# Norm in two halves, turned gate products and a lighter VectorE queue in the prologue of an attention and mixture-of-experts kernel

## The reference

```
xn = layernorm(x)
q, k, v = heads(xn @ W.T)                         # 16 heads of 16
std = softmax(causal(q k' / 4)) v                 # plain attention
gauss = exp(-0.5 |q - pos|^2 / scale^2), dirp = tanh((q - pos) . dirn)   # 8 splats a head, same for k
gsa = softmax(causal(q k'/4 + 0.3 * (amp gauss_q gauss_k' + 0.4 * amp gauss_q dirp_q (gauss_k dirp_k)'))) v
attn = ((1-blend) std + blend gsa) @ Wo.T
logits = xn @ gate_w.T                            # 16 experts, top 2, capacity 128
w = sqrt(softplus(logits)); y = sum_k w_k * W2[e_k] (silu(W1[e_k] xn) * (W3[e_k] xn))
shared = Ws2 (silu(Ws1 xn) * (Ws3 xn))
out = x + attn + y + shared
```

## Time and profile before

| | us |
|---|---|
| median of 3 runs | 358.19 |
| lowest, highest | 356.69, 360.31 |
| the profiled execution, whole | 356.44 |
| its span (first to last instruction) | 354.7 |
| PE, DVE, ACT, POOL busy in it | 316.1, 235.8, 201.4, 39.7 |
| mean granted TensorE clock | 0.981 |

### The profile page before, as it was taken

The page is one execution under the profiler, slowest core; times in us unless marked ns, Lnnn a source line. Parts: engine busy times, 40 slices in busy tenths (PEclk is TensorE's granted clock), DMA queues, the critical chain, the costliest instruction groups (busy, mean ns, idle before and its releaser), DMA issues.

```text
span 354.7 us, 6091 instructions
## 1 busy us (share of the span) xinstructions
PE 316.1 (89%) x2064; PEld 161.2 (45%) x2064; DVE 235.8 (66%) x735; ACT 201.4 (57%) x300; POOL 39.7 (11%) x59
## 2 busy tenths in 40 slices
PE   0899898977779999999999999999999999999984
PEld 0548533223423455444544455445445554445352
DVE  4858776499997568964766567665766568666424
ACT  1696277575645576654565465555555545647730
POOL 7300000000020000111111111102110004444000
PEclk9998998999978999999999999999999999999999
DMA  7424353224146303635455536554554443222011
GB/s 243 132 43 65 57 99 88 55 43 67 30 65 167 73 2 48 137 112 138 112 140 116 161 87 146 129 143 100 128 145 134 102 80 78 59 72 60 7 59 59
DMA packets 25790, 33.54 MB, mean 95 GB/s; under 512 B 4636, under 2 KB 18556, under 8 KB 25756
## 3 DMA queue, kind: packets, MB, share of 16 engines
q1 hardware_dynamic: 24056, 28.85, 35.3%
q0 software_dynamic: 1536, 4.20, 4.3%
q10 hardware_dynamic: 164, 0.07, 0.1%
HBM read 16.15 MB, written 4.26 MB: 58 GB/s over the span
## 4 chain that ended last, share of the span: by engine, by line
PE 44%; DVE 5%; ACT 2%; issue 2%; DMA 1%; SPq 1%; DVEq 0%
PE ps L897 12%; PE ps L813 6%; PE ps L822 5%; PE ps L879 5%; PE ps L867 4%; PE ps L775 4%; PE ps L852 2%; DMA stage<-split 1%; PE ps L817 1%; PE ps L870 1%; ACT arena_p L670 1%; DVE mx L1215 1%; ACT small L682 1%; PE ps L826 1%; PE ps L801 1%
## 5 line engine op out<-in xcount | busy, mean ns | idle before, releaser
L670 ACT ACTIVATE arena_p<-ps 128x1024 f32<-128x1024 f32 (+1 forms) x192 | 148.0, 808 | 49.6 <-PE ps L879 29.2
L897 PE MATMUL ps<-arena_p,v_full 128*32 128x512 f32 (+3 forms) x768 | 72.6, 496 | 0.0
L1183 DVE CUSTOM_DVE_ANT_0 ps<-ps,mask_r 128x128 f32<-128x128 f32 (+3 forms) x128 | 61.7, 501 | 11.6 <-PE ps L775 6.9
L775 PE MATMUL ps<-stage 96*128 96x512 bf16 (+3 forms) x160 | 50.6, 354 | 8.1 <-DVE mx L1215 3.7
L867 PE MATMUL ps<-stage 98*128 98x512 bf16 (+1 forms) x192 | 51.6, 333 | 3.7 <-ACT arena_p L670 3.0
L1215 DVE TENSOR_REDUCE mx<-ps 128x1 f32<-128x512 f32 x64 | 43.9, 686 | 14.5 <-PE ps L775 14.1
L879 PE MATMUL ps<-stage 98*128 98x512 bf16 (+1 forms) x192 | 47.2, 334 | 2.5 <-ACT arena_p L670 2.3
L452 POOL DMA_INDIRECT wt<-xn_scratch,ids_sb x16 | 15.3, 954 | 235.3 <-PE ps L801 107.6
L897 PEld LDWEIGHTS ps<-arena_p,v_full 128*32 128x32 f32 x768 | 20.1, 110 | 34.6 <-issue 30.0
L775 PEld LDWEIGHTS ps<-stage 96*128 96x128 bf16 x160 | 15.6, 99 | 29.6 <-issue 22.2
L675 ACT ACTIVATE small<-ps 128x176 f32<-128x176 f32 x24 | 7.6, 317 | 37.2 <-PE ps L813 37.2
(11 more groups left out here) (199 smaller groups left out, 374.2 us busy)
## 6 DMA issues: line engine op xcount, KB each, us to landing
w_sb<-in_w_dram SPq DMA_DIRECT2D x16, 352.0 KB
stage<-split SPq DMA_DIRECT2D x48, 96.0 KB
stage<-split SPq DMA_DIRECT2D x96, 32.0 KB
stage<-split SPq DMA_DIRECT2D x48, 64.0 KB
arena_o<-in_w_dram SPq DMA_DIRECT2D x16, 176.0 KB
ye_scratch<-wt SPq DMA_DIRECT2D x16, 128.0 KB, 2.6
stage<-split SPq DMA_DIRECT2D x32, 48.0 KB
acc<-in_x_dram SPq DMA_DIRECT2D x2, 512.0 KB, 4.7
```

What stands on the lines that cost most here:

```text
L670: A(to, ps[:, 1 + 2 * s:3 + 2 * s, off:CH], ACT.Exp, scale=SCALE).then_inc(done, 1)
L775: ins = M(b[:, 0:n1 - n0], qs[0:KR, pr, h, it * P:(it + 1) * P], ks[0:KR, pr, h, n0:n1], start=True, stop=True)
L897: ins = M(ps[c:c + 2 * HD, 0, off:CH], v_full[:, jb + s, g * GH + h, :], of, start=jb + s == 0, stop=end or last, skip_group_check=last an ...
L1183: return V.tensor_tensor_reduce(row, row, mask_r[:, CH - row.shape[1]:CH], 1.0, NEG, ALU.add, ALU.max, to)
```

## The change

- x arrives in four DMAs of 256 rows. Mean, variance, root and normalisation are done for rows 0 to 511, then for 512 to 1023. One q projection of the first half is put on PE between the transposes of the halves. Waits on ACT's count now go through `emptied_at`.
- The squares of q and k for heads 0 to 7 move from ACT (read from PSUM) to DVE (`square`, four of 128 x 512, read from SBUF).
- The gate products are turned round: `gateT` uses the gate weights as the stationary side (four matmuls of 16 x 512), DVE copies both 16-row blocks to `pv_sb`, and eight small transposes (`gate`, 0 and 1) bring them back to tokens on partitions.
- The third parts of the features (at = 2, 3) move from DVE to GpSimd.
- On DVE, `gate` now stands before the first maximum, `plus_one` after two tasks of the maxima, and a part of the old `plus_one` (`corrected`) in front of the copy of shift 0.
- For the maxima made in the prologue and in turns 0 and 1 (`g <= EARLY`), PE adds the mask by one more matmul of 128 x 128 (48 in all) and DVE uses the plain maximum.
- PE: the first `proj1` stands in front of shift 0; v tasks 2 and 3 stay between the maxima. ACT: the table changes for Ln, Sqrt and Exp are in other places, all before the last two `proj1` are emptied.

```diff
-        PRO = [("xnT", (k, tq)) for tq in range(NC) for k in range(KD)]
-        PRO += [("proj", (s, tc)) for s in range(2) for tc in range(NC)] + [("par", m) for m in range(2)]
-        PRO += [("feat", (tc, w)) for tc in range(NC) for w in range(2)] + [("gate", 0)] + [("v", n) for n in range(NT // 2)]
+        PRO = [("xnT", (0, 0)), ("xnT", (1, 0)), ("proj", (0, 0)), ("xnT", (0, 1)), ("xnT", (1, 1)),
+               ("proj", (1, 0)), ("proj", (0, 1)), ("proj", (1, 1))]
+        PRO += [("par", m) for m in range(2)]
+        PRO += [("feat", (tc, w)) for tc in range(NC) for w in range(2)] + [("gateT", 0), ("v", 0)] + [("gate", tq) for tq in range(NC)]
+        PRO += [("v", n) for n in range(1, NT // 2)]
...
+        EARLY = 1
...
 # GpSimd, after its constants
+            for at in (2, 3):
+                pool.wait_ge(second_rest, at + 1)
+                pool.wait_ge(second_part, at + 1)
+                nc.gpsimd.tensor_tensor(part_of(at, 2), rest_of_x(at), part_of(at, 1), ALU.subtract).then_inc(part_done[at], 1)
...
 # SyncE
-            for n in range(NC):
-                sp.dma_start(acc[:, n * TC:(n + 1) * TC, :],
+            for n in range(NT // 2):
+                sp.dma_start(acc[:, 2 * n:2 * n + 2, :],
...
 # ScalarE
-                if m == 0:
-                    A(sq[m][:, s, cols], b, ACT.Square).then_inc(squares, 1)
...
+            root_of(0)
+            act.wait_ge(norm_ready, 1)
+            A(NRM, NSQ, ACT.Sqrt).then_inc(norm_root, 1)
+            evacuate(("xnT", (0, 0)))
+            evacuate(("xnT", (1, 0)))
+            root_of(1)
+            exponentials()
             evacuate(("proj", (0, 0)))
...
+            evacuate(("v", 3))
+            evacuate(("proj1", (0, 0)))
+            shift_rows(act, -1, 0, 0)
             evacuate(("proj1", (0, 1)))
...
             A(g_[10][:, :, :], g_[11][:, :, :], ACT.Sqrt).then_inc(gate_act, 1)
+
+            A(PRE_, GG, ACT.Exp)
+            evacuate(("proj1", (1, 0)))
             evacuate(("proj1", (1, 1)))
...
 # TensorE
+                elif kind == "gateT":
+                    for k in range(KD):
+                        for tq in range(NC):
+                            last = M(b[32 * tq:32 * tq + E, :], gw_sb[:, k, :], xnT[:, k, tq * CH:(tq + 1) * CH],
+                                     start=k == 0, stop=k == KD - 1)
...
-                                start=True, stop=True)
+                                start=True, stop=g > EARLY)
+                        if g <= EARLY:
+                            ins = M(b[:, n1 - P:n1], ident_b[:, :], mask_n, start=False, stop=True)
...
                 if n in (AB, 2 * AB - 1):
-                    prologue(n_v + 2 + n // 4)
+                    prologue(n_late + n // 4)
+                elif t[0] == "shift":
+                    prologue(n_p)
...
 # VectorE
+            moments(0)
+            variance(0)
...
+            normalise(0)
+            moments(1)
+            variance(1)
+            normalise(1)
...
+            for s, tc in ((0, 0), (1, 0), (0, 1)):
+                square(s, tc)
             rest_of(0)
+            square(1, 1)
...
             third_of(1)
+            n = PRO.index(("gateT", 0))
+            dve.wait_ge(pro_full, n + 1)
+            for tq in range(NC):
+                rows = slice(32 * tq, 32 * tq + E)
+                ins = V.tensor_copy(pv_sb[rows, :], ps[rows, n % PB, :])
+            ins.then_inc(pro_dve, 1)
             product(0)
             rest_of(2)
             rest_of(3)
-            third_of(2)
-            third_of(3)
...
-            for t in max0:
-                aux(-1, t)
             gate()
-            aux(-1, ("shift", 0))
-            for t in PRE1[0:2]:
+            for t in max0[0:2]:
                 aux(-1, t)
             plus_one()
-            for t in PRE1[2:5]:
+            for t in max0[2:]:
+                aux(-1, t)
+            corrected()
+            aux(-1, ("shift", 0))
+            for t in PRE1[0:1]:
                 aux(-1, t)
             softplus()
-            for t in PRE1[5:]:
+            for t in PRE1[1:]:
                 aux(-1, t)
```

More of the change, by code:

```diff
@@ L927, in own @@
                     pe.wait_ge(own_rows, g + 1)
-            n_v, n_p = PRO.index(("v", 0)), PRO.index(("proj1", (0, 0)))
-            for n in range(n_v + 2):
+            n_late, n_p = PRO.index(("v", 2)), PRO.index(("proj1", (0, 0)))
+            for n in range(n_late):
                 prologue(n)
```

114 lines of the change are left out of this document (62 added, 52 removed).

## The result

The change made the kernel slower: 360.32 us (358.77 to 361.56, five runs) against 357.57 (355.83 to 360.31, five runs). The ratio is **1.0086 [1.0049, 1.0122]** (the bracket is the 95% interval), some 3.1 us. The profiled execution took 360.32 us with a span of 358.5.

What follows compares the result with a forecast made beforehand. PE and DVE wait by turns in the prologue, then DVE sets the pace, with SyncE's queue capping any lead. 356.44 - 1.8 (lead) + 0.8 (masks) - 0.3 (DVE's gain) = 355.1 us, 356.9 off the median; range 353.0 to 361.0.

Steps and rivals of the forecast that it cites:

- The third parts on GpSimd: Prologue: passes of 2.2 us each from about 34.3; maxima from 36.9, mhl ready at 42.05 against 42.38 before.
- To the first turn: End of prologue: first scores at 50.3, not 52.17; first exponential at 51.1 against 53.49; lead 2.2 us.
- Held until 36.5, then the maxima begin at 36.9: Gate operations on DVE held by GpSimd only until 36.5; maxima start at 36.9 instead of 36.62.
- The port decides, slower: Rival: GpSimd passes over 3 us delay the maxima, PE stands and its clock falls; 361.0 us; chance 0.15.
- ACT has its table changes behind it by then: Before the first turn: last projection emptied at 50.2, first exponential at 51.1 against 53.49.
- Gate products turned round: Prologue: 2.7 us on PE against 3.7, score rows at 33.6, not 36.25; product at 30.6, 2.3 us later.
- The head: Kernel's start: PE ends projections 1.5 us ahead, at about 19.2; with ACT's relief worth 0.1 us at the features.
- What is late next: SyncE: Feature-row queue on SyncE runs 1.5 us later, free for shift 1 at 61.1; at most 1.8 us of lead passes.
- cap of 1.8 us: Limit SyncE's sending of shift 1 puts on the lead: at most 1.8 us ahead of the matmul at 65.90.
- The masks on PE: 48 matmuls in prologue and turns 0 and 1: cost 0.8 us on PE, DVE gains 0.3 us.
- Mostly beside DVE: The 12 mask matmuls in the prologue fall mostly beside DVE's work; each costs PE 0.1 us.
- The footing: Profiled execution before lies 1.75 us below the median of three, 358.19; forecast 355.1 becomes 356.9 on the median.

Runs made afterwards that it cites:

- g1: The change with GpSimd's second third-part pass waiting until both gate operations on VectorE are done; ratio to the kernel before 1.0044.
- f1: The change with v 2 and v 3 on PE in front of the first score rows; ratio to the kernel before 1.0031.
- u1: The change with the third feature parts back on VectorE; ratio to the kernel before 0.9995.
- a1: The change with the gate's arithmetic behind the first maxima and ACT's table changes behind its evacuations; ratio to the kernel before 1.0026.
- p1: The change with product(0) in front of gateT's two copies on VectorE, nothing else; ratio to the kernel before 1.0019.
- h1: The kernel before with the new head alone (quarters of x, norm by halves, early projection, squares on VectorE); ratio to before 1.0018.
- o1: The change with the old head (x in halves, one norm, transposes ahead of projections, squares on ACT); ratio to the kernel before 1.0120.
- o2: v1 with the old head (x in halves, one norm, squares on ACT); ratio to the kernel before 0.9932.
- n1: v1 without the mask matmuls on PE, VectorE's masked maxima everywhere; ratio to the kernel before 0.9928.
- v1: The change with gate arithmetic behind the maxima, product(0) before gateT's copies, ACT's table changes behind its evacuations; 354.46 us, ratio to before 0.9915.
- b1: The kernel before with only the third feature parts moved to GpSimd; ratio to before 0.9990.
- u2: The change with the gate's arithmetic behind the first maxima, third parts still on GpSimd; ratio to the kernel before 0.9987.

## Why the prediction was wrong

I forecast 356.9 us, a gain of 1.3; measured is a loss of some 3.1. The 360.3 lies inside my range of 353.0 to 361.0, and the ratio in the 1% either way that had 0.70, because both were wide: the direction was wrong. The step that failed is **The third parts on GpSimd**, and with it **To the first turn**.

- *The pass's size was right*: 2.13 us against 2.2. *Its place was right too*: `rest_of(3)` ends 12.3 us after the features, as summed. What failed is the sentence "Held until 36.5, then the maxima begin at 36.9". I let both gate operations through between two passes and made only `plus_one` wait for the second. The |x| operation did wait for the first pass, and when it got through, the second pass was already queued ahead of max(x, 0). The maxima began 16.6 us after the features, not 14.9. g1 forces the order that I had assumed and gets 14.7. The Trainium skill (SBUF — State Buffer, "Who interferes with whom") says that whoever issues first gets the shared ports for its whole instruction, and the trace agrees, twice in a row: 1.94 and 2.14 us. Had I charged the second pass to the second operation as well, my own numbers would have given 34.3 + 2 x 2.2 = 38.7, or 16.7 us after the features, where 16.6 was measured.
- *A cost that I had in a rival and not in the forecast*: PE stood, and the clock fell behind it to a mean of 0.64. "The port decides, slower" had this mechanism, with v 3 at twice its time, at 361.0 us; the measured 360.3 is nearest to it. I set its threshold at 3 us a pass because I had the maxima wait for nothing behind the first pass. It decided at 2.13, and 0.15 was too little. f1 and u1 show PE's part: in f1 equally late maxima with PE at work, and in u1 maxima only 1.05 us sooner with a stand of 2.27, bring the first scores 2.6 and 2.7 us back.
- *ACT's table changes*: the sentence "ACT has its table changes behind it by then" failed too. I had the last projection end at 49.5 and emptied at 50.2; in the change it ends at 53.40 and is emptied at 55.15, behind a table load at 52.67, with PE standing 1.34 us. In a1, where the emptying goes ahead of the changes, that stand is 0.24. So the first scores came 32.5 us after the features, where my sum had 28.3.
- **Gate products turned round**: gateT 1.90 (1.75 forecast), the eight transposes 0.43 (0.95), product 8.65 us after the features (8.6), PE at the score rows 11.2 after them (11.6). As summed, but for the transposes. What I hadn't seen is where PE's lead comes from: about half of it is v 0 and v 1 no longer running at a fallen clock (5.31 us before, 3.98 now). All four profiles with the old gate products have this fall, and the fourteen with `gateT` don't; no run turns the products round alone. But I used the delay only to say where the third parts' 2.38 us went. As a term of its own it is 0.7% of the kernel (p1): it delays the maxima and SyncE at once, and no run separates the two.
- **The head**: the last xn ends at 12.18 (12.3), but the early projection takes 3.65 us and not 1.72. PE's end at 20.2 instead of 19.2 moves the third square and `rest_of(0)`, and the features come at 22.77, not 22.0. I took the projection's time from a stretch in which PE had been working since 10.07. PE's lead was to be 20.9 - 19.2 = 1.7 us, not the 1.5 I wrote. The step's conclusion, that the lead is worth next to nothing, holds (h1, o1, o2).
- **What is late next: SyncE** is right, and never came to bear in the change itself. a1 and n1 show it: PE waits 1.65 and 0.92 us for shift 1. But my cap of 1.8 us was mis-summed: I wrote that the rows take 1.7 us from the start of the second issue and counted from its end. In a1 PE goes on 1.75 us after that start (61.98 + 0.68 to 64.41), which from 61.1 gives 2.4 us ahead of 65.90.
- **The masks on PE**: 0.5 us net was forecast. Alone they cost 1.0045, 1.6 us [0.5, 2.7]. "Mostly beside DVE" is wrong for the kernel before: 0.73 us of it lies in the prologue, on PE's path. v1 against n1 shows no such cost in the times.
- The footing was sound: the profiled execution after is the median of its runs.

The best kernel here is v1: 354.46 us (351.07 to 355.25, twelve runs), 0.9915 [0.9882, 0.9948] of before. It keeps every part of the change, with the gate's arithmetic behind the maxima, the product ahead of gateT's copies and ACT's table changes behind its evacuations.

## What to carry to other kernels

When work moves to GpSimd, list every VectorE operation that can issue while its passes run, and charge each one of a kind that was held here with a whole pass if a further pass is already queued; put reductions from PSUM there and the rest behind. A moved wait costs twice if another engine has work left behind it: ask what PE could do meanwhile, since the run with v 2 and v 3 ahead had its first scores 2.6 us sooner with the wait left in place (about half a per cent of the time, with intervals that overlap). And an operation that feeds both a DMA queue and the maxima (here the product) goes ahead of copies that nothing needs yet.

## What was not expected of the hardware

- PE's first work runs at half speed, though the granted clock of the stretch reads 1.00: in thirteen profiles the projection at 10.5 us took 3.34 to 3.75 us, where four such matmuls take 1.8 at 14.9 us. The time of the recovery differs by about 1 us from run to run (the eight transposes at 14 us took 1.04 to 1.92). With the old head 16 transposes come first, in 3.76 to 3.92 us, and the 16 matmuls behind them take 7.03 to 7.64, so little of it falls on them. Nor does full speed come sooner for a PE that starts sooner: its last slow matmul starts at 13.2 to 15.8 us with the new head, where PE starts at 7.5, and at 13.3 to 14.6 with the old one, where it starts at 10. The stretch of the change's profile (columns as in the earlier trace rows):

```profile
10.00:14.20 4.20, 3.66 (x6) 1.58 (x7) 3.62 (x12) 2.23 (x6) 1.90 (x3) 1.00 0.30 103
```

- A scalar_tensor_tensor whose two inputs both lie in SBUF is held by GpSimd's pass just as a tensor_scalar is; reductions from PSUM ran beside it at their usual 1.14 us for four. No row of the kernel before had shown the former.
- A GpSimd pass of 128x1024 with two inputs and a bf16 result takes 2.1 us (4.21 to 4.26 for two, in twelve profiles, and 2.13 and 2.12 apart), where VectorE's takes 1.19.
- How long TensorE's clock is down differs between executions of one kernel, and some 2 us go with it (g1: 355.9 to 357.4 at a mean of 0.986 and 0.988, 359.0 to 359.6 at 0.981). A difference of half a per cent between two single profiles can therefore be a fall of the clock in one of them, as at 80 to 90 us, where before's profile has 1.00 and those of the change, b1, g1, f1 and u2 have 0.83.
